# Attention, two-way Mamba and routed FFN on one core: work moved between POOL, DVE, ACT and PE, loads and first attention rearranged

## What is computed

```python
Q, K, V = Wq @ x + bq, Wk @ x + bk, Wv @ x + bv
t = to_tokens(softmax(Q.T @ K / sqrt(128)) @ V + x)          # attention

n = ln(t)                                                    # forward, and over reversed tokens
for direction in (fwd, bwd):
    xc, z = split(n @ in_proj.T)                             # 256 channels each
    xc = silu(causal_conv4(xc) + conv_b)
    dt, Bm, Cm = split(xc @ x_proj.T)                        # 16, 16, 16
    dt = softplus(dt @ dt_w + dt_b)
    h[s] = exp(dt * A[s]) * h_before[s] + dt * xc * Bm[s]    # scan over 1024 tokens, 16 states s
    y = (sum_s(h[s] * Cm[s]) + xc * D) * silu(z)
    m += y @ out_w.T
t = t + m + leaky_relu((ln(m) * g + b) @ w1.T + b1) @ w2.T + b2

n2 = ln(t)
w = n2 @ wr + br
kept = tokens with the 511 largest w
t = t + n2 + where(kept, w * (gelu(n2 @ f_w1 + f_b1) @ f_w2 + f_b2), 0)
```

## Time and profile before

| | us |
|---|---|
| runs of the kernel, median of 3 (lowest to highest) | 8342.78 (8341.23 to 8348.9) |
| profiled execution, span from the first to the last instruction (no other time of it is given) | 8342.4 |
| PE busy | 7778.2 (93%) |
| DVE busy | 7384.7 (89%) |
| ACT busy | 7209.6 (86%) |
| POOL busy | 7494.7 (90%) |
| mean granted TensorE clock, share of full | 0.987 |

### The profile page before, as it was taken

One profiled execution on the slowest core, in us unless ns is written; L12 is line 12 of the kernel. 1 busy time (PEld: TensorE's weight loads), 2 busy tenths in 40 slices (PEclk: granted clock), 3 DMA queues, 4 the chain that ended last, 5 costly groups with the idle time before them and its releaser, 6 DMA issues. The chain is left out here.

```text
span 8342.4 us, 152469 instructions
## 1 busy us (share of the span) xinstructions
PE 7778.2 (93%) x53376; PEld 6086.4 (73%) x53376; DVE 7384.7 (89%) x10476; ACT 7209.6 (86%) x12224; POOL 7494.7 (90%) x7020
## 2 busy tenths in 40 slices
PE   6999999999999999999999999999999999999986
PEld 4777777777777777777777777777777777777765
DVE  4899999999899999999988999999899999889885
ACT  5898898898888898888888888988889888889874
POOL 3999999999999999999899999999899999899985
PEclk9999999999999999999999999999999999999998
DMA  1222222222222222222222222222222222222221
GB/s 51 75 65 81 76 75 75 72 72 77 75 74 75 72 72 78 75 74 75 68 76 75 75 75 72 73 77 75 73 75 72 73 76 76 73 71 71 77 71 35
DMA packets 322661, 604.29 MB, mean 72 GB/s; under 512 B 42017, under 2 KB 45026, under 8 KB 321890
## 3 DMA queue, kind: packets, MB, share of 16 engines
q1 hardware_dynamic: 321890, 594.45, 23.0%
HBM read 556.55 MB, written 20.97 MB: 69 GB/s over the span
## 5 line engine op out<-in xcount | busy, mean ns | idle before, releaser
L1096 POOL TENSOR_TENSOR g<-h,c_all 128x1024 f32<-128x1024 f32 x2048 | 4858.1, 2372 | 455.0 <-PE ps L530 250.7
L864 ACT ACTIVATE da<-dt,a_neg 128x512 f32<-128x512 f32 x4096 | 2792.6, 714 | 201.2 <-DVE h L1197 195.6
L1197 DVE TENSOR_TENSOR_SCAN h<-da,ps 128x512 f32<-128x512 f32 x2048 | 2423.9, 1208 | 377.6 <-PE ps L526 219.1
L1197 DVE TENSOR_TENSOR_SCAN h<-da,h,ps 128x512 f32<-128x512 f32 x2048 | 2552.0, 1269 | 127.6 <-PE ps L526 48.6
L526 PE MATMUL ps<-ident,ub 128*128 128x128 f32 x16384 | 2397.3, 276 | 240.4 <-DVE h L1197 221.8
L526 PEld LDWEIGHTS ps<-ident,ub 128*128 128x128 f32 x16384 | 1878.9, 142 | 890.3 <-issue 495.6
L530 PE MATMUL ps<-ident,g 128*128 128x128 f32 x16384 | 2253.8, 275 | 14.5 <-POOL g L1096 11.0
L530 PEld LDWEIGHTS ps<-ident,g 128*128 128x128 f32 x16384 | 1897.9, 142 | 462.6 <-issue 431.4
L1082 POOL TENSOR_SCALAR ub<-u_tok,b_tok 128x256 f32<-128x256 f32 x4096 | 1929.3, 486 | 183.1 <-ACT u_tok L953 99.5
L876 ACT ACTIVATE ub<-u_tok,b_tok 128x256 f32<-128x256 f32 x4096 | 1839.6, 498 | 136.9 <-PE ps L526 121.3
L853 ACT ACT_TABLE_LOAD x446 | 572.2, 1283 | 7.9
(11 more groups left out here) (130 smaller groups left out, 9368.8 us busy)
## 6 DMA issues: line engine op xcount, KB each, us to landing
c_all<-c_rows SPq DMA_DIRECT2D x2048, 256.0 KB, 3.1
x_in<-in_x SPq DMA_DIRECT2D x32, 512.0 KB, 5.6
t_old<-t SPq DMA_DIRECT2D x32, 512.0 KB, 4.4
out<-tile_b SPq DMA_DIRECT2D x32, 512.0 KB, 2.9
c_rows<-rows SPq DMA_DIRECT2D x128, 32.0 KB, 2.9
w_conv<-in_conv_rows SPq DMA_DIRECT2D x1, 512.0 KB
f_w<-in_f_w SPq DMA_DIRECT2D x2, 256.0 KB
hid<-in_in_proj SPq DMA_DIRECT2D x1, 256.0 KB
```

The costliest lines, as they stand in the source:

```text
L864: act.activation(da[:, n % 2, half, :], dt[:, slot, half, :], ACT.Exp, scale=a_neg[:, r, half, s:s + 1]).then_inc(da_made, 1)
L1096: pool.tensor_tensor(g[:, n % 2, :, :], h[:, n % 2, :, at:at + BANK], c_all[:, n % RING, :].unsqueeze(1).to_broadcast([P, NH, BANK]), ALU.mult
L1197: dve.tensor_tensor_scan(h[:, n % 2, half, at:at + BANK], da[:, n % 2, half, :], ps[:, DB + half, :], before, ALU.mult, ALU.add).then_inc( ...
```

## The change

- The gate moves from POOL to DVE. The skip now writes its sum to PSUM, and the gate reads it there and writes `xc`. PE's matmuls into `Y` now wait for the gate.
- The addition of `n2` (residual) by POOL goes; DVE adds it when it copies the result out, in place of ACT's copy.
- The addition of `b2` by POOL goes; PE puts the bias into the banks ahead of the second MLP matmul, as it already does for `f_b2`. Both biases now use two rows of weights, partition 0 for the first bank and 32 for the second.
- The bias of dt comes in as a 17th row of `w_dt`, against a row of ones made by the copy of `rows` (now 96 rows, Identity with a bias column).
- The softplus is max(x, 0) + ln(1 + exp(-|x|)): ACT takes |x| from PSUM, exp and ln; DVE does one instruction of 1024 where it did four of 512.
- `y` is copied from PSUM by ACT, at slots of its own.
- LN 1 is applied by POOL instead of ACT.
- All loads but the first 7 are issued by SP at the start of the first turn.
- The first attention uses four pairs of banks instead of two, in another order.
- All slot tables have new numbers.

Core of the diff:

```diff
-    AT_SKIP = (6, 75, 137, 201)
-    AT_GATE = ((8, 8), (72, 93), (148, 148), (221, 225))
+    AT_YKEEP = (3, 64, 130, 192)
+    AT_SKIP = (11, 74, 136, 202)
+    AT_GATE = ((14, 15), (75, 79), (136, 137), (203, 205))
...
-    AT_MT = (23, 25)
-    AT_B2 = (82, 113)
-    AT_T1OLD = 34
+    AT_MT = (40, 45)
+    AT_T1OLD = 40
...
+    FIRST_PAIRS = 4
...
-                return Y if i % 2 and not now else X
+                return X if now else (X, Y, DB, YA)[i % FIRST_PAIRS]
...
-                            elif c == 0 and (now or i > 1):
-                                pe.wait_ge(t1_made, since(t1_made, i if now else i - 1))
+                            elif c == 0 and (now or i >= FIRST_PAIRS):
+                                pe.wait_ge(t1_made, since(t1_made, i if now else i - FIRST_PAIRS + 1))
...
-                    for dst, src in loads:
-                        sp.dma_start(dst, src).then_inc(loaded, 16)
...
+                    if not now and nxt:
+                        sp.wait_ge(rows_zeroed, 1)
+                        with nc.allow_non_contiguous_dma(reason="weights, once"):
+                            for dst, src in loads:
+                                sp.dma_start(dst, src).then_inc(loaded, 16)
...
+                    def bias_banks(bias):
+
+                        for c in range(NCH):
+                            at_row = slice(c * QUAD, c * QUAD + 1)
+                            mm(by_block(ps[:, X + c, :]), ones_row[at_row, :],
+                               bias[at_row, :].unsqueeze(1).to_broadcast([1, QB, C]), True, False)
...
                             if k in closed:
-                                pe.wait_ge(y_skip, since(y_skip, closing(k, NH, NH)))
+                                pe.wait_ge(y_gated, since(y_gated, closing(k, NH, NH)))
...
                                 pe.wait_ge(hid1_leaky, since(hid1_leaky, HM))
+                                bias_banks(b2)
...
-                            if i % QB == 0:
-                                mm(by_block(ps[:, X + i // QB, :]), ones_row[:],
-                                   f_b2[:].unsqueeze(1).to_broadcast([1, QB, C]), True, False)
+                                bias_banks(f_b2)
...
+                        if at == AT_YKEEP[k]:
+                            act.wait_ge(y_made, since(y_made, DS * k + left))
+                            if k - 1 in closed or joined:
+                                act.wait_ge(y_turned, since(y_turned, closing(k - 1, 1, 1)))
+                            act.activation(y_tok[:].rearrange("p b d -> p (b d)"), banks(YA), ACT.Copy).then_inc(y_kept, 1)
...
-                            act.activation(rows[:], ps[0:XROWS, Y, :], ACT.Copy).then_inc(rows_kept, 1)
+                            act.activation(rows[:], ps[0:XROWS, Y, :], ACT.Identity, bias=one_col[0:XROWS, :]
+                                           ).then_inc(rows_kept, 1)
+                        if at == AT_DTABS[k]:
+                            act.wait_ge(dt_made, since(dt_made, prep(k, NH, NH)))
+                            act.activation(dt[:, side, :, :], ps[:, Y:Y + NH, :], ACT.Abs).then_inc(dt_abs, 1)
...
-                            act.activation(dt[:, side, :, :], dt[:, side, :, :], ACT.Exp).then_inc(dt_exp, 1)
+                            act.activation(dt[:, side, :, :], dt[:, side, :, :], ACT.Exp, scale=-1.0).then_inc(dt_exp, 1)
...
-                            act.activation(out_s, banks(X), ACT.Copy).then_inc(out_kept, 1)
...
+                                pool.tensor_scalar(dst[:, i, :], src[:, i, :], rstd[:, n, i:i + 1], shift[:, n, i:i + 1],
+                                                   ALU.mult, ALU.add).then_inc(ln_made[n], 1)
...
-                                pool.tensor_tensor(xc[:, slot, half, :], xc[:, slot, half, :], sz[:, slot % NCH, half, :],
-                                                   ALU.mult).then_inc(y_gated, 1)
...
-                                pool.tensor_tensor(res[:, some, :], res[:, some, :],
-                                                   b2_rows[:].unsqueeze(1).to_broadcast([P, QB, C]), ALU.add
-                                                   ).then_inc(b2_added, 1)
...
-                                half_sum(res, res, n2, part).then_inc(base_made, 1)
...
-                        dve.tensor_copy(y_tok[:].rearrange("p b d -> p (b d)"), banks(YA)).then_inc(y_kept, 1)
...
-                                dve.scalar_tensor_tensor(xc[:, slot, half, :], xc[:, slot, half, :],
+                                dve.scalar_tensor_tensor(ps[:, Y + half, :], xc[:, slot, half, :],
                                                          d_skip[:, r, half:half + 1], ps[:, Y + half, :],
                                                          ALU.mult, ALU.add).then_inc(y_skip, 1)
+                        for half in due(AT_GATE[k], at):
+                            dve.wait_ge(y_skip, since(y_skip, closing(k, NH, half + 1)))
+                            if k:
+                                dve.wait_ge(z_kept, since(z_kept, gates(k - 1, NH, half + 1)))
+                            dve.tensor_tensor(xc[:, slot, half, :], ps[:, Y + half, :], sz[:, slot % NCH, half, :],
+                                              ALU.mult).then_inc(y_gated, 1)
...
-                            for half in range(NH):
-                                dve.scalar_tensor_tensor(ps[:, Y + half, :], ps[:, Y + half, :],
-                                                         b_dt[:, r, half:half + 1], dt[:, side, half, :],
-                                                         ALU.add, ALU.max).then_inc(dt_max, 1)
+                            dve.scalar_tensor_tensor(ps[:, Y:Y + NH, :], ps[:, Y:Y + NH, :], 0.0, dt[:, side, :, :],
+                                                     ALU.max, ALU.add).then_inc(dt_max, 1)
...
+                        if at == AT_OUTKEEP:
+                            dve.wait_ge(out_turned, since(out_turned, 1))
+                            dve.wait_ge(ln_kept[2], since(ln_kept[2], 1))
+                            dve.tensor_tensor(out_s, banks(X), n2c, ALU.add).then_inc(out_kept, 1)
```

More of the change, by code:

```diff
@@ L140, in due @@
+    FIRST_T1 = tuple(FIRST + 11 + 4 * i for i in range(8))
+    SETUP = FIRST + 26
     def due(slots, g):
@@ L1145, in aside @@
                                                    ).then_inc(earlier_made, 1)
-                            for part in due(AT_BASE, at):
-                                pool.wait_ge(ln_made[2], since(ln_made[2], NB))
-                                half_sum(res, res, n2, part).then_inc(base_made, 1)
                         if nxt and at == LN_POW[0]:
@@ L1373, in dve_turn @@
                         scan(n, 0)
-                        if n % DS == 1 and (n > DS or last):
-                            keep_y(n // DS - 1)
                         aside(SLOTS * n)
@@ L1380, in dve_turn @@
                         aside(SLOTS * n + 3)
-                    if last and not now:
-                        keep_y(-1)
                     if not now:
```

281 lines of the change are left out of this document (134 added, 147 removed).

## The result

The changed kernel takes 8152.3 us (median of 4 runs, 8140.7 to 8153.2) against 8342.8: 0.9765 of the time, 95% interval 0.9752 to 0.9779. Forecast were 8158. The profiled execution took 8152.0 with a span of 8150.3, mean granted clock 0.988 (before 0.987).

The account below looks back on a forecast made before the run. POOL was taken to set the pace in quarters one and two, PE in three, DVE in the last; 8342.4 - 16 - 13 + 1.3 - 2 - 155 (5.0 per image on 31) = 8158 us, forecast band 8070 to 8250, range 8020 to 8300.

Parts of the forecast that it names:

- head: Start of the kernel before the images' turns: earlier PE start -16 us, first attention -13, table load +1.3.
- the tail: End of the kernel: b2 bias adds 1.3 us, feed-forward bias loses 1.0, gate 2 x 0.6: 0 in all.
- Loads: Head: with weight loads behind the barrier, PE starts near 6.8 us instead of 22.78: -16 us, or -12.
- First attention: Head: a block of queries takes 4.9 us instead of 6.53: -13 us, ends -9 and -14.
- First image: The first image, which has only the later quarters, gets 2 us shorter.
- Prices of the instructions: Per-image busy time from instruction lengths: POOL -12.4 us, DVE -4.4, ACT +1.4, PE +0.3.
- the slower rival: PE's first matmul of each quarter waits for skip and gate on DVE: 11.0 us per image lost, 8498 us; chance 0.08.
- by quarter, each against its longest engine: Ordinary turn in four quarters of 16 steps, each limited by its busiest engine: -2.5, -1.7, 0, -0.8 us, sum -5.0.
- a sign of its being wrong: POOL idle before the multiplication by C for more than 14 us per image, released by DVE.
- POOL held whenever DVE gates: Steady part: DVE's gates hold POOL 8 x 0.68 = 5.4 us per image, eating the 5.0 gain; 8313 us, chance 0.04.

Follow-up runs that it names:

- the sum on DVE: Changed kernel with the fused kept-weight instruction and the residual sum at slots 40 and 45 on VectorE instead of GpSimd: 8151.8 us, ratio 0.9776.
- the filler: Changed kernel plus an unread 128x512 product on GpSimd at the eight gates' slots, gates staying on VectorE: 8325.0 us, ratio 0.9988.
- the fused form over 128x8: Changed kernel with one VectorE scalar_tensor_tensor for the kept weight in place of nine instructions (is_kept and eight products): 8144.4 us, ratio 0.9762.

## Why the prediction was right, and which steps failed

- **The sum**: 8158 forecast, 8152 measured. Per image -5.0 forecast, -5.1 measured in the 29 turns; head -16 - 13 + 1.3 = -27.7, measured -26.6.
- **The end**: from the last image's load to the last instruction 613.7 us became 593.8, 20 less, where the forecast has two images at 5 and 0 for the tail. The last turn, which has no next attention beside it, gives 10.2 of them (253.2 to 243.0 from the g ahead of its first step to its last g). So the total is nearer to the forecast than its terms are, and no run explains this one.
- **Loads**: right. 18.5 us with the loads of the new kernel, 16.3 of them seen as PE's earlier start (22.78 to 6.52).
- **First attention**: right in kind, mis-sized twice. A block takes 4.38 us (4.9 forecast: the lengths of three rows were added up, but each starts some 0.15 before the one ahead of it ends), yet the part brings 11.7 instead of 13, as the pipeline's ends are not covered.
- **First image**: -2 forecast, +1.6 measured; no run explains it.
- **Prices of the instructions**: gate 0.66 us (0.68), bias pair 1.16 and 1.03 (1.26), norm on POOL 0.43 (0.35 taken, end 0.47). Net busy time of the turn: POOL -11.7 (-12.4), ACT +1.0 (+1.4), DVE -3.9 (-4.4). DVE carries 2.2 us that nobody foresaw: `is_kept` went from 172 to 2373 ns at the median, as its new slot meets g.
- **PE waiting for the gate** (the slower rival): 1.4 us of w_conv's weight loads and 13.9 of w_in's in the whole run, half a microsecond per image. The rival's condition did not occur with the gate on DVE; with the gate on POOL at these slots it did, 4.3 us per image.
- **The step that failed** is "by quarter, each against its longest engine". It gave -2.5, -1.7, 0, -0.8; measured were -3.25, -0.93, -1.56, +0.58, and that the sum agrees is luck: the errors cancel. A quarter is not one resource: 2 us less POOL in quarter 1 gave 0.0 (the sum on DVE, which also put 1.5 us on DVE), 2.2 more gave 1.8 (the filler), 1 us less DVE in a quarter that DVE filled to 98% gave 0.2. And the gate's move alone, in the old slots, made the kernel slower by 206 to 218 us. What the text named as a sign of its being wrong appeared, too: POOL idles 21.5 us per image in front of g, 16.9 of them released by DVE (5.4 before). The granted clock stands nowhere in the sum; in the changed kernel it was 0.988 in the mean, before 0.987, so it does not decide between these two, but it adds to the loss of the runs that hold PE up.
- **What stands in its place**: a step is 3.24 us where nothing stands in the way, and the insertions that were tried were paid in full in such a step and partly or not at all in a long one. The gain needs three things together: the gate off POOL (230 us in the new slots), the gate from PSUM (172), and slots that spread what DVE and PE then have to do. The new slots and the other parts with the gate on POOL are 0.5% slower than before, the gate on DVE in the old slots 2.5 to 2.6%; only both together gain. These amounts overlap and do not add up to the 190. What the additions of `n2` and `b2`, the new softplus and the copy of `y` by ACT bring in the changed kernel is not shown: no run undoes them there.
- **The rival "POOL held whenever DVE gates"** got 0.04 because g's length was even the earlier trace rows (its time is 8312, not 8313, by its own sum). That row could not speak: no instruction of DVE with two SBUF tensors as inputs ran often in the kernel before. The hold is real, and the change avoids it for the gate by where the operand lies. What the Trainium skill warns of there (Perfetto Trace Analysis, "Optimizing Scalar/DVE Operations") holds for such operands, by the trace, and not for a gate that reads PSUM.

## What to carry to other kernels

Where engines hand a loop to one another, cut the time at the loop's own heartbeat before pricing a move: busy shares of a long stretch do not say which insertion is free. When work moves from GpSimd to VectorE, try it with one operand in PSUM, and look in the trace whether anything small on VectorE (here `is_kept`, with a single SBUF operand) now lasts as long as GpSimd's instruction beside it. Move the work together with the slots that it needs on the engine that takes it; try the move without the new slots, and the slots without the move, before crediting either. Compare several turns, with the granted clock beside each, before pricing a step from one.

## What the runs showed of the hardware

- A product on DVE with two SBUF operands that met a POOL instruction lasted past its end and held the next one; an addition, too, took up to 0.94 us beside POOL instead of 0.68. The gate took 0.68 us with one operand in PSUM; with both in SBUF it took 1.23 at the median in the new slots, and 0.68 at the median but 4.45 at most in the old ones. Tiny ones stood still too: `is_kept`, with one SBUF operand and no accumulator, and the fused form over 128x8, with two, took 2.37 us each from start to end of a g. Comparisons that also write an accumulator ran beside g at their usual length, here 0.87 us:

```profile
2805.62 0.87 DVE L1321 TENSOR_SCALAR_CACHE_REDUCE compared<-w_row,w_col 128x640 bf16<-128x640 f32 x1
2813.88 2.37 DVE L1332 TENSOR_SCALAR is_kept<-rank 128x8 f32<-128x8 f32 x1
```
```profile
2805.20 2.36 POOL L1120 TENSOR_TENSOR g<-h,c_all 128x1024 f32<-128x1024 f32 x1 [3.64 <-DVE h L1214]
2813.86 2.36 POOL L1120 TENSOR_TENSOR g<-h,c_all 128x1024 f32<-128x1024 f32 x1 [3.98 <-DVE h L1214]
```

- Two bias matmuls on rows 0 and 32 of the weights into neighbouring banks take 1.03 to 1.16 us together; one alone took 1.12.
- The granted clock fell to its lower level (0.50, 1.2 GHz) for 3.4 or 6.8 us at a time behind idle time of PE: 1.81 us in quarter 1 of the changed kernel, 2.42 in the last quarter with the gate on POOL, 4.43 in front of the projection at slot 13. The same 1.81 us stand in turns without a fall, so what decides is open. Eight transposes of 128x128 took 1.91 us at the lower level and 1.04 to 1.09 at the upper one.
